# A message-passing kernel: the copy of x into the output in interleaved runs of 16 rows

## The reference

```python
h = relu(layernorm(x))
deg = segment_sum(ones, src)                     # how often a node is a source
deg_inv = where(deg > 0, rsqrt(max(deg, 1)), 0)
norm = deg_inv[src] * deg_inv[dst]
h_j = h[dst]                                     # gathered row of each edge
c_e = comps[edge_type]                           # 4 numbers for each edge
msg = einsum('ebd,bdf->ef', c_e[:, :, None] * h_j[:, None, :], bases)
msg = msg * alpha[edge_type] * norm[:, None]
out = x + segment_sum(msg, src)                  # add each message to its source's row
```

## Time and profile before

| | us |
|---|---|
| median of 3 runs | 830.52 (830.2 to 843.87) |
| the profiled execution | 832.09 |
| its span, first to last recorded instruction | 830.0 |
| busy: PE, DVE, ACT, POOL | 583.1, 595.5, 369.4, 538.8 |

### The profile page before, as it was taken

One profiled execution on the slowest core, in us unless ns is written; L12 is line 12 of the kernel. 1 busy time (PEld: TensorE's weight loads), 2 busy tenths in 40 slices (PEclk: granted clock), 3 DMA queues, 4 the chain that ended last, 5 costly groups with the idle time before them and its releaser, 6 DMA issues.

```text
span 830.0 us, 13837 instructions
## 1 busy us (share of the span) xinstructions
PE 583.1 (70%) x3922; PEld 423.3 (51%) x3922; DVE 595.5 (72%) x2613; ACT 369.4 (45%) x1493; POOL 538.8 (65%) x404
## 2 busy tenths in 40 slices
PE   1219576773775887777777968858886987798760
PEld 1117474653643665545555646646664665665430
DVE  4119677775767997666787869868886897898630
ACT  0103452624254354454564545555555555555520
POOL 1208778672300577778877787788786878677775
PEclk9659878888898899899898989998999899999995
DMA  4968799899601344444444445444544353534332
GB/s 146 351 233 298 261 342 332 294 341 333 210 8 52 64 87 77 75 89 90 79 87 86 86 76 90 90 87 76 94 84 89 53 113 58 96 55 77 33 32 25
DMA packets 56527, 108.89 MB, mean 131 GB/s; under 512 B 9291, under 2 KB 48216, under 8 KB 55636
## 3 DMA queue, kind: packets, MB, share of 16 engines
q0 software_dynamic: 34496, 25.72, 23.3%
q10 hardware_dynamic: 1600, 51.20, 17.2%
q1 hardware_dynamic: 20356, 31.10, 12.4%
HBM read 94.89 MB, written 64.61 MB: 192 GB/s over the span
## 4 chain that ended last, share of the span: by engine, by line
DMA 38%; DVE 16%; issue 14%; PE 12%; POOL 11%; ACT 7%; SPq 1%; POOLq 0%; ACTq 0%; DVEq 0%
DMA out_dram<-acc,scatter_idx 17%; DMA rows<-in_x_dram,dst_i 7%; POOL out_dram L375 6%; DMA edge_row<-edge_rows 6%; DMA src_rows<-rows 5%; POOL rows L355 4%; PE pst L714 4%; DVE masked L462 4%; PE pst L733 3%; DVE turned_hot L456 3%; DVE part_sum L497 3%; ACT scratch L591 3%; PE pst L700 2%; DMA rows<-edge_rows 2%; ACT scratch L583 2%
## 5 line engine op out<-in xcount | busy, mean ns | idle before, releaser
L375 POOL DMA_INDIRECT out_dram<-acc,scatter_idx x196 | 312.2, 1593 | 139.5 <-ACT acc L638 61.3
L355 POOL DMA_INDIRECT rows<-in_x_dram,dst_i x196 | 224.6, 1146 | 144.0 <-PE pst L700 56.0
L714 PE MATMUL pst<-table_bits,turned_hot 128*128 128x198 f16 x1568 | 183.9, 266 | 78.5 <-DVE masked L462 74.7
L733 PE MATMUL pst<-bases_sb,h_turned 128*128 128x512 f32 x392 | 217.9, 639 | 0.0
L714 PEld LDWEIGHTS pst<-table_bits,turned_hot 128*128 128x128 f16 x1568 | 149.5, 106 | 103.9 <-issue 55.9
L497 DVE SCALAR_TENSOR_TENSOR part_sum<-pst,coef,part_sum 128x128 f32<-128x128 f32 x392 | 115.4, 344 | 105.2 <-ACT part_sum L628 104.6
L741 PEld LDWEIGHTS pst<-rows,same 128*128 128x128 f32 x392 | 75.3, 206 | 184.4 <-issue 153.4
L462 DVE SCALAR_TENSOR_TENSOR masked<-iota_h,lo,pst 128x198 f32<-128x198 f16 x392 | 141.2, 415 | 7.1 <-PE pst L714 7.0
L741 PE MATMUL pst<-rows,same 128*128 128x128 f32 x392 | 86.5, 305 | 69.4 <-ACT acc L638 63.5
L628 ACT ACTIVATE part_sum<-pst,coef 128x128 f32<-128x128 f32 x196 | 71.0, 362 | 135.3 <-PE pst L733 134.0
L583 ACT ACTIVATE scratch<-rows 128x128 f32<-128x128 f32 x196 | 57.8, 297 | 157.8 <-DMA rows<-in_x_dram,dst_i 157.8
(11 more groups left out here) (71 smaller groups left out, 410.4 us busy)
## 6 DMA issues: line engine op xcount, KB each, us to landing
out_dram<-in_x_dram ACTq DMA_DIRECT2D x50, 1000.0 KB
src_row<-src_rows SPq DMA_DIRECT2D x27, 512.0 KB, 3.9
edge_row<-edge_rows SPq DMA_DIRECT2D x49, 256.0 KB, 4.9
rows<-in_x_dram,dst_i POOLq DMA_INDIRECT x196, 4.6
out_dram<-acc,scatter_idx POOLq DMA_INDIRECT x196
rows<-edge_rows SPq DMA_DIRECT2D x14, 175.0 KB
src_row<-src_rows SPq DMA_DIRECT2D x1, 448.0 KB, 3.7
out_dram<-in_x_dram SPq DMA_DIRECT2D x1, 304.0 KB, 3.3
```

Of the source, the lines that this page charges most:

```text
L355: pool.indirect_dma_start(row(t), None, x, bass.IndirectOffsetOnAxis(ap=dst_i[:, t:t + 1], axis=0)) \
L375: pool.indirect_dma_start(out, bass.IndirectOffsetOnAxis(ap=scatter_idx[:, t:t + 1], axis=0), acc[:, t % ACC_RING, :], None, bounds_check= ...
L714: last = pe.matmul(pst[:, LOOK + t % 2, k * LO:(k + 1) * LO], turned_hot[:, g % 2, c, k * W + j * P:k * W + (j + 1) * P], table[:, c * LO: ...
L733: pe.matmul(pst[:, PRODUCT + t % 4, :], h_turned[:, g % 2, j, :], bases_sb[:].rearrange("d b f -> d (b f)"), start=True, stop=True).then_i ...
```

## The change

A piece is no longer 2,000 consecutive rows. The rows are cut into 25 blocks of 4,000, a block into 250 runs of 16 rows (8,192 B), and one piece takes the even runs of a block, the next one the odd runs: 125 runs in a piece, again 1,024,000 B. Two pieces instead of eight are issued at the beginning, and three instead of two ahead of each group's statistics. The number of pieces stays 50, so the last three are issued ahead of `stats(15)`.

```diff
     COPIES = 50
-    COPY_ROWS = N // COPIES
-    COPIES_FIRST = 8
-    assert COPIES * COPY_ROWS == N
+    COPY_RUN = 16
+    COPY_ROWS = 2 * N // COPIES
+    COPIES_FIRST, COPIES_EACH = 2, 3
+    assert COPIES // 2 * COPY_ROWS == N and COPY_ROWS % (2 * COPY_RUN) in (0, COPY_RUN)
...
             def copy():
                 if copy_at[0] < COPIES:
-                    a = copy_at[0] * COPY_ROWS
+                    a = copy_at[0] // 2 * COPY_ROWS
+                    odd = copy_at[0] % 2
                     copy_at[0] += 1
-                    flat_out, flat_x = (y[a:a + COPY_ROWS, :].rearrange("r d -> (r d)") for y in (out, x))
-                    act.dma_start(flat_out.rearrange("(q e) -> q e", q=32), flat_x.rearrange("(q e) -> q e", q=32)) \
-                        .then_inc(copied, 16)
+                    runs_out, runs_x = (y[a:a + COPY_ROWS, :].rearrange("(q r) d -> q (r d)", r=COPY_RUN)[odd::2, :]
+                                        for y in (out, x))
+                    act.dma_start(runs_out, runs_x).then_inc(copied, 16)
...
             for g in range(STATS_BEFORE):
                 for i in range(types_before(g - 1), types_before(g)):
                     keep_coef(i)
-                copy()
-                copy()
+                for _ in range(COPIES_EACH):
+                    copy()
                 stats(g)
```

## The result

The changed kernel takes 1050.2 us (median of 4 runs, 1047.49 to 1053.22) against 830.36 us, a ratio of 1.266 with a 95% interval of 1.2596 to 1.2724. The forecast was 1080 us, in a range of 1000 to 1160. The profiled execution took 1047.49 us, its span is 1045.4 us.

A forecast was written before the change was run, and what follows sets the result against it. Transfers bound 13 to 217 us, GpSimd's scatters the time from 270. With five engines holding ScalarE, histogram ends at 450 us, plus 68 us to the first scatter-add (518), plus 559.3 gives 1077, forecast 1080 us, range 1000 to 1160.

The forecast's parts named there:

- The number of engines: Copy of x into out: a piece of 125 runs is carried by five DMA engines instead of 16.
- The rate: Copy on five engines: 24.1 GB/s an engine, 8.5 us a piece, 425 us for 50; bounds 7.97 and 10.9 us.
- the other traffic: Gathers, type rows and first edge rows on the same engines: 43 us, so the copy lands at 481 us.
- The hold of ScalarE: ScalarE's issuing stalls behind full engines; 50th piece issued at 444 us, delaying keep_coef and histogram to about 450 us; chance 0.60.
- rival A: Issuing does not hold ScalarE; GpSimd waits at line 365 until 481 us: 1032 us in all; chance 0.21.
- Some 100: Issuing is held while some 100 descriptors stand before one engine; at 26 a piece, about four pieces in flight.
- The lookups: Histogram's end to first scatter-add: 68 us instead of 92.8, leaving 3 us of the stuck edge row's 27.66.
- the loop behind: From the first scatter-add to the end: 559.3 us, carried over unchanged.
- The small parts: Issuing costs nothing; earlier index stores start the histogram some 20 us earlier, worth nothing; SyncE's issues perhaps held, a few us.
- the signs that the prediction named for itself: 6,500 packets on q10, busy share near 0.35, issues of several us, TensorE waiting for coef_parts, first scatter-add past 500 us.
- B: Rival: pieces spread over all engines, smaller packets free type and edge rows: 792 us, 770 to 830; chance 0.13.
- C: Rival: 8 KB packets are slow, 18.75 GB/s an engine, 11.8 us a piece: end 1192 us; this or worse 0.06.

The follow-up runs named there:

- e1: Changed kernel with runs of 25 rows for 16 (80 of 12,800 B a piece, 16 engines), same order: 830.0 us, 0.989 of the kernel before.
- e2: Changed kernel with runs of 20 rows for 16 (100 of 10,240 B a piece, 10 engines), same order: 860.6 us, 1.029 of the kernel before.
- e3: Changed kernel with runs of 80 rows for 16 (25 of 40,960 B a piece, five engines), same order: 1049.8 us, 1.257 of the kernel before.
- e6: Changed kernel with runs of 5 rows (400 of 2,560 B, 16 engines) and the order of before (8, then 2): 805.8 us, 0.969 of before.
- e5: Changed kernel's 125 runs of 8,192 B with the order of before (8 pieces first, then 2): 1023.0 us, 1.228 of the kernel before.
- e7: Changed kernel with runs of 5 rows (400 of 2,560 B, 16 engines), keeping the new order (2, then 3): 830.0 us, 0.997 of before.
- e10: Changed kernel with runs of 5 rows (400 of 2,560 B), two pieces first, two with each group: 797.6 us, 0.947 of the kernel before.
- e4: Kernel before, contiguous pieces, with the new order alone (two pieces first, then three): 841.9 us, 1.006 of the kernel before.
- e9: Changed kernel with runs of 5 rows (400 of 2,560 B), four pieces first, two with each group: 806.9 us, 0.961 of the kernel before.

## Why the prediction was right

**The number of engines.** The step that decides was right to the word: 6,500 packets. It came from counting SyncE's completion words (1,528) against the divisors of the row counts, and e1, e2, e3, e6 show the same rule for copies within DRAM: 80 and 400 runs give 16 engines, 100 give 10, 125 and 25 give five.

**The rate was mis-sized.** I took 24.1 GB/s an engine, 8.5 us a piece, and 0.86 us a piece for the other traffic. q10's 11.6% of 16 engines' 1045.4 us are 388 us on each of five: 7.76 us a piece, 26.4 GB/s. The first of these windows is a stretch in which nothing but the copy ran, and its 134 GB/s are 26.8 an engine:

```profile
243.70:257.70 14.00, 0.00 (x0) 0.00 (x0) 0.00 (x0) 0.00 (x0) 0.00 (x0) 0.50 0.32 134
13.00:442.00 429.00, 122.26 (x1192) 109.36 (x1191) 138.23 (x560) 70.58 (x373) 107.18 (x93) 0.65 0.38 149
```

Both are above my upper bound of 25.7, which came from a window with other traffic in it. The Trainium skill gives about 27 GiB/s (29.0 GB/s) an engine in "DMA: Bandwidth & Descriptors", "Specifications"; this trace stays 8% under that. The issues of 7.01 us do not give the rate: two of them fill the first window, and 134 GB/s drained only 1.83 pieces in it. The other traffic was sized right: a share of 0.38 of 429 us is 163 us an engine, less 121 of the copy are 42 us, 43 forecast. From 13.8 to 406.95 us, by my count of 46 pieces, are 8.55 us each for the forecast's 9.36, of which 7.76 are the copy and 0.79 the rest: ScalarE was free 37 us earlier than the forecast 444 us.

**The hold of ScalarE** was right, and it is the forecast's difference from rival A: the issues last 7 us at the median, keep_coef(11) and turn_types(13) come right behind the last piece, and the copy's landing (440 us; 481 forecast) is not waited for. e5 shows it as a cause: with the same five engines, moving pieces in ScalarE's order moved the histogram from 392.3 to 323.9 us. That descriptors are what fills up was argued from two rows of SyncE's queue; e2 and e3 show it. "Some 100" and four pieces fit the changed kernel (98), but pieces of 6 or 11 descriptors were held from 73 and 77 on, so one fixed number of descriptors is not the whole rule either, and what sets it stays open. One step was misread without harm: I let the histogram end with turn_types(13), at 450 us. table_bits waits only for the histogram's own matmuls and began at 392.3 us; what ScalarE's last piece held up was turn_types(13) at 410.8 us, and the lookups behind it.

**The lookups** took 10 us more than forecast: 78.1 us from the release of turn_types(13) to the first scatter-add for 68, since I gave back almost all of the edge row's 27.66 us as if all of it had been in the chain's way. VectorE's waits for edge rows ahead of the first scatter-add were 11.2 us in all before and are 1.9 in the changed kernel: 9 us to win, where I had counted 24.7. With -37 for ScalarE, -2 for stats(15) and keep_coef, +10 here and -3 in the loop behind, the forecast span of 1077 comes to the measured 1045.

**The small parts.** That the earlier stores are worth nothing here was right: they landed in 15.8 us, and the histogram was then held by ScalarE. SyncE was hardly held by ScalarE's full queue: four edge rows were issued in 1.92 us, two src rows in 5.91 us. Of the signs that the prediction named for itself one did not come: the first scatter-add was to be past 500 us and was at 488.9.

**The rivals.** A would have shown issues of 0.6 us; it is out. B, the pieces on all engines, is out by the packet count, and its estimate of 792 us for small packets on 16 engines was too good for the change's own order (e1 and e7: 830) and near what the order of before or fewer pieces first gives (806 to 798). C is out: 8 KB packets ran at 26.4 GB/s an engine, not 18.75.

## What to carry to other kernels

Before cutting a DRAM to DRAM copy into strided runs, factor the number of runs: here 125 instead of 80 or 400 runs took eleven of 16 engines out and cost 27% of the kernel. Count a queue's packets against the shapes; the surplus is how many engines took part. Then ask which engine issues the copy and what stands behind it in its order: here a queue that drained slowly stopped its issuer, well before anyone waited for the data. The duration of a held issue is not the time that a piece takes; the rate comes from the queue's share or a quiet window. Short packets on all 16 engines beat long ones with the order of before (e6), and the fastest version also had few pieces at the beginning (e10), but e4 and e9 show that fewer pieces ahead do not pay each time.

## What the runs showed that I had not expected

- By q10's time on each engine, a copy on five engines moves 26.4 GB/s on each (388 us), on ten in e2 26.1, and on all 16 of the kernel before 22.4 (142.8 us). In the windows five engines and the other traffic have 144 GB/s in all, ten in e2 274, 16 in e1 344. Eleven sixteenths fewer engines cost less than eleven sixteenths of the rate.
- Two kernels with five engines, e3 and the changed one, end within 0.4 us of each other with histograms 69 us apart: a stall that is removed can uncover another of the same length.
- 2,560 B packets cost the copy only 6% of engine time: q10's share is 18.8% of 801.9 us in e6, 150.8 us an engine, against 142.8 us with 64,000 B.
